# Nine hat products of a strip divided between VectorE and GpSimd, and a second group of sampled values taken by VectorE, in a fused residual network with a deformable convolution

## What is computed

```python
def _deform_conv(x, offsets, w_def, stride, pad):
    off = offsets.reshape(B, K2, 2, Ho, Wo)
    dy, dx = (off[:, :, 0], off[:, :, 1])
    ...
    py = hs[None, None, :, None] + iy[None, :, None, None] + dy
    px = ws[None, None, None, :] + ix[None, :, None, None] + dx
    y0 = jnp.floor(py)
    x0 = jnp.floor(px)
    wy = py - y0
    wx = px - x0
    ...
    val = gather(y0, x0, (1 - wy) * (1 - wx))
    val = val + gather(y0, x0 + 1, (1 - wy) * wx)
    val = val + gather(y0 + 1, x0, wy * (1 - wx))
    val = val + gather(y0 + 1, x0 + 1, wy * wx)
    return jnp.einsum('bckhw,ock->bohw', val, w_def.reshape(Cout, C, K2))
offsets = _conv2d(x, w_off, b_off, STRIDE, PAD)
...
x = x + _L0_conv_ref(_gn(x), ...)
x = x + _L1_conv_ref(_gn(x), ...)
```

## Time and profile before

| | us |
|---|---|
| median of 3 runs (lowest, highest) | 1302.1 (1301.43, 1303.63) |
| the profiled execution's own time | 1300.54 |
| its span, first to last instruction | 1298.7 |

### The profile page before, as it was taken

How to read it: one execution, slowest core, us unless ns; L and a number is a source line. 1 busy time by engine, 2 the same in 40 slices (tenths; PEclk the granted TensorE clock), 3 DMA queues, 4 the chain that set the end, 5 groups by cost and what they waited for, 6 DMA issues and landing times.

```text
span 1298.7 us, 42328 instructions
## 1 busy us (share of the span) xinstructions
PE 1061.0 (82%) x17334; PEld 681.5 (52%) x17334; DVE 887.3 (68%) x1379; ACT 669.6 (52%) x901; POOL 61.9 (5%) x87
## 2 busy tenths in 40 slices
PE   0799999987593999999965867888878887888884
PEld 0234546664241454447742325777767776776764
DVE  4877762334985878751517947888878887888870
ACT  0532433112175334332113476888878887888871
POOL 0000000000051000000000350000000000000000
PEclk9999999999795999999998876999999998999998
DMA  9000022110585000202305345443433443444331
GB/s 198 1 1 2 2 94 67 42 27 4 134 202 150 1 1 2 91 6 67 67 1 123 93 142 152 137 133 112 135 117 110 122 135 102 125 128 124 114 86 36
DMA packets 96466, 109.83 MB, mean 85 GB/s; under 512 B 10127, under 2 KB 85735, under 8 KB 94616
## 3 DMA queue, kind: packets, MB, share of 16 engines
q1 hardware_dynamic: 87816, 101.73, 28.6%
q10 hardware_dynamic: 8464, 5.37, 1.9%
HBM read 74.85 MB, written 32.22 MB: 82 GB/s over the span
## 4 chain that ended last, share of the span: by engine, by line
issue 44%; PE 41%; DVE 5%; POOL 2%; ACT 2%; DMA 2%; SPq 1%; POOLq 0%; DVEq 0%; ACTq 0%
PE psum L832 22%; PE psum L901 13%; PE psum L965 3%; DMA xm<-x 2%; DVE v L1626 2%; PE psum L942 1%; SPq L529 1%; POOL offr L2003 1%; POOL offp L2007 1%; ACT xm L1377 1%; PE psum L979 1%; PE psum L923 1%; DVE xm L1792 1%; PE psum L932 1%; DVE stats L1795 1%
## 5 line engine op out<-in xcount | busy, mean ns | idle before, releaser
L832 PE MATMUL psum<-v,u 64*64 64x512 f32 x3072 | 336.8, 597 | 17.7 <-DVE v L1626 12.7
L1449 ACT ACTIVATE dist<-psum 128x1024 f32<-128x1024 f32 x288 | 288.9, 1025 | 54.1 <-PE psum L1028 39.1
L832 PEld LDWEIGHTS psum<-v,u 64*64 64x64 f32 x3072 | 148.2, 134 | 204.8 <-issue 188.1
L1839 DVE TENSOR_SCALAR dist<-dist 128x1024 f32<-128x1024 f32 x288 | 201.9, 701 | 77.1 <-ACT dist L1449 75.5
L1075 PE MATMUL psum<-hat,win 64*64 64x144 f32 x4096 | 199.5, 318 | 32.7 <-DVE outt L1875 18.2
L1849 DVE TENSOR_TENSOR hat<-dist 128x512 f32<-128x512 f32 x288 | 194.8, 685 | 0.3
L1148 PE MATMUL psum<-val,wdefs 64*64 64x256 f32 x1944 | 166.0, 395 | 33.0 <-ACT val L1452 24.1
L1075 PEld LDWEIGHTS psum<-hat,win 64*64 64x64 f32 x4096 | 152.7, 135 | 66.3 <-issue 64.7
L1452 ACT ACTIVATE val<-psum 128x864 f32<-128x864 f32 (+3 forms) x230 | 146.5, 675 | 34.6 <-PE psum L1075 22.7
L1028 PE MATMUL psum<-offs,sels 61*64 61x256 bf16 x2304 | 139.1, 284 | 21.4 <-issue 11.2
L1148 PEld LDWEIGHTS psum<-val,wdefs 64*64 64x64 f32 x1944 | 91.1, 136 | 48.1 <-issue 44.6
(11 more groups left out here) (144 smaller groups left out, 1097.2 us busy)
## 6 DMA issues: line engine op xcount, KB each, us to landing
win<-pixd SPq DMA_DIRECT2D x256, 68.0 KB
win<-pixd SPq DMA_DIRECT2D x128, 136.0 KB
raw<-x SPq DMA_DIRECT2D x16, 512.0 KB, 7.4
x1d<-xm SPq DMA_DIRECT2D x16, 512.0 KB, 6.0
pixd<-turned SPq DMA_DIRECT2D x64, 128.0 KB, 3.9
x1t<-x1d SPq DMA_DIRECT2D x63, 128.0 KB, 2.8
out<-outt SPq DMA_DIRECT2D x63, 128.0 KB, 2.6
offd<-offp SPq DMA_DIRECT2D x48, 128.0 KB
```

The lines of the kernel that those rows point to most:

```text
L832: mm = pe.matmul(o, u4[half, i, v, ky, :], V[half, at:at + CHUNK, cg, v, :], start=start, stop=stop, skip_group_check=True)
L1449: act.activation(dist_at(j, n), psum[:, slot:slot + 2, :], ACT.Abs).then_inc(dist_abs, 1)
L1839: dve.tensor_scalar(d, d, 1.0, 1.0, ALU.min, ALU.subtract).then_inc(hats_made, 1)
```

## The change

Three of the nine products of a strip (taps 1, 4 and 7) are issued by POOL, with a semaphore of their own (`prod_pool`); DVE keeps six. Whoever waited for products now waits for the one of the two semaphores that counts that product, and PE's group 0 for both. Group 4 of the values, 128x576, goes from ACT to DVE, behind the hats of tap 8. The core of the diff:

```diff
-ACT_GROUPS = [0, 1, 3, 4, 5]
-DVE_GROUPS = [2]
+ACT_GROUPS = [0, 1, 3, 5]
+DVE_GROUPS = [2, 4]
+POOL_UNITS = [1, 4, 7]
+DVE_UNITS = [0, 2, 3, 5, 6, 8]
...
+        def product_made(s, n):
+
+            if n in POOL_UNITS:
+                return prod_pool, len(POOL_UNITS) * s + (POOL_UNITS.index(n) + 1)
+            return prod_dve, len(DVE_UNITS) * s + (DVE_UNITS.index(n) + 1)
...
                 if g == 0:
                     pe.wait_ge(win_in[j], count)
-                    pe.wait_ge(prod_dve, UNITS * (s + 1))
+                    pe.wait_ge(prod_dve, len(DVE_UNITS) * (s + 1))
+                    pe.wait_ge(prod_pool, len(POOL_UNITS) * (s + 1))
...
-                    act.wait_ge(prod_dve, UNITS * q + (m_ + 1))
+                    act.wait_ge(*product_made(q, m_))
...
                     if not last:
                         hats(s + 1, 1 - j, n)
-                        if n > 0:
+                        if n - 1 in DVE_UNITS:
                             product(s + 1, 1 - j, n - 1)
...
             for n in range(UNITS):
                 hats(0, 0, n)
-                product(0, 0, n)
+                if n in DVE_UNITS:
+                    product(0, 0, n)
...
+            def products(s, j):
+
+                for n in POOL_UNITS:
+                    if n == POOL_UNITS[0] and not (isinstance(s, int) and s < 2):
+                        pool.wait_ge(vals_made, GROUPS * (s - 1))
+                        settled(pool)
+                    pool.wait_ge(hats_made, UNITS * s + (n + 1))
+                    pool.tensor_tensor(*product_of(j, n), ALU.mult).then_inc(prod_pool, 1)
+
+            products(0, 0)
+            products(1, 1)
+            with pool.Fori(1, STRIPS // 2) as h:
+                products(2 * h, 0)
+                products(2 * h + 1, 1)
```

More of the change, by code:

```diff
@@ L370, in build @@
         prod_dve = sem("prod_dve")
+        prod_pool = sem("prod_pool")
         vals_made = sem("vals_made")
@@ L488, in general, with product_of @@
                     end()
+        def product_made(s, n):
+            if n in POOL_UNITS:
+                return prod_pool, len(POOL_UNITS) * s + (POOL_UNITS.index(n) + 1)
+            return prod_dve, len(DVE_UNITS) * s + (DVE_UNITS.index(n) + 1)
+        def product_of(j, n):
+            d = dist_at(j, n)
+            lo = TAP_PITCH * n + n % K
+            to = hat[:, j, lo:lo + BANK].rearrange("p (b n) -> p b n", b=IMAGES)
+            return to, d[:, :, 0:PS * HALF_W], d[:, :, PS * HALF_W:]
         def group_taken(s, g):
@@ L1499, in edge_absolute @@
                 if e:
-                    act.wait_ge(prod_dve, UNITS * STRIPS)
+                    act.wait_ge(prod_dve, len(DVE_UNITS) * STRIPS)
+                    act.wait_ge(prod_pool, len(POOL_UNITS) * STRIPS)
                 act.activation(dist[:, DIST_RING - 1, :, 0:K * W0], psum[:, 0:2, 0:K * W0], ACT.Abs).then_inc(edge_abs, 1)
@@ L1845, in product @@
                 dve.wait_ge(hats_made, UNITS * s + (n + 1))
[L1846 to L1849, removed]
+                dve.tensor_tensor(*product_of(j, n), ALU.mult).then_inc(prod_dve, 1)
             def edge_product(e):
```

## The result

| | before | with the change |
|---|---|---|
| median of 10 runs, us | 1301.81 | 1304.96 |
| lowest, highest | 1296.02, 1303.63 | 1303.02, 1306.8 |
| profiled execution: span, us | 1298.7 | 1304.2 |

The ratio to before is 1.0028, with a 95% interval from 1.0014 to 1.0041: slower, by 2 to 5 us. The forecast was slower by 13.5. The direction held and the size did not: 3.15 us is a quarter of what I had summed.

What follows compares the result with a forecast made beforehand. Bound: a chain of engines waiting in turn. A strip loses 0.50 - 0.10 = 0.40 us, 12.0 us over 30 strips, plus 1.5 at the start: 1300.5 + 13.5 = 1314.0, plus 1.6 to the median, 1315.5 us; range 1300 to 1328.

Steps and rivals of the forecast that it cites:

- What bounds the kernel: Engines wait in turn; PE stands still 18.2 us for DVE's result and 24.1 us for ACT's last copies.
- The price of POOL's product: On DVE ahead of the result: 0.60 us removed, 1.10 added by blocked hats, result 0.50 late in each strip.
- the upper bound for two products: A product on DVE and one on POOL were priced as excluding each other, for the whole 1.16 us.
- the first rival: On DVE and POOL: two products run side by side, only hats are blocked; 1302 us, chance 0.12.
- The second: Rival: POOL gets in only where DVE waits, so the result comes 0.60 us earlier; 1291.5 us, chance 0.13.
- The third: Rival: DVE becomes the bound, all three blocks count, 0.9 to 1.0 us a strip; about 1331 us, chance 0.15.
- Taps 4 and 7 at nothing: On DVE behind the result: the blocked hats of taps 5 and 8 added nothing to the strip's sum.
- The products together: POOL's three products: 0.50 us for each of 30 strips, plus 1.5 us for blocked hats ahead of any strip.
- Group 4, "I credit 0.1 us a strip": At the strip's end ACT loses one copy, about 0.62 us; 0.1 was credited, the other 0.52 covered by PE.
- is done in time: DVE's copy of group 4 (0.7 us), behind the hats of tap 8, would be done at about 1017.3.
- The sign: For the whole kernel: slower at chance 0.72, faster 0.17, same 0.11.

Runs made afterwards that it cites:

- e7: Kernel before, with POOL multiplying the hats of tap 1 once more into an unread buffer, nothing taken from DVE; 1328.94 us against 1302.08, ratio 1.0199.
- e8: e5 with the result moved one place forward on DVE, ahead of the product of tap 3; ratio to before 0.9931.
- e4: Changed kernel with only the products of taps 4 and 7 on POOL and group 4 back on ACT; ratio to before 1.0034.
- e1: Changed kernel with group 4 back on ACT, so only the products of taps 1, 4 and 7 move to POOL; 1313.52 us against 1300.92, ratio 1.0085.
- e2: Kernel before with only the copy of group 4 moved to DVE, all nine products staying on DVE; 1308.3 us against 1300.92, ratio 1.0061.
- e5: e2 with DVE copying group 4 directly behind the hats of tap 8, ahead of the product of tap 7; ratio to before 0.9987.

## Why the prediction was right and wrong

**What bounds the kernel: right.** The time is decided on DVE's order between the hats of tap 1 and the result, and by PE's waits for result and copies. e7 and e8 show that from both sides: 1.09 us more there cost 26 us, one place less brought about 7.

**The price of POOL's product: right, to 0.01 us.** I summed 1.10 added, 0.60 removed, 0.50 late. Measured: 1.10 (e7), and 5.31 against 4.82, 0.49. The choice of the upper bound for two products, argued from doubled reading, was right too (1.63 us at 778.34), so the first rival fell. (It is the first rival, not the second as the prediction has it, that goes with two products side by side.) The second fell with it: POOL never waited longer than one product of DVE. The third did not come either: DVE still waits 51.9 us for ACT between the first and the 30th result.

**Taps 4 and 7 at nothing: nearly right.** e4 measures 4 us (2 to 7) for them.

**The products together: over-priced.** Without the credit for group 4 my sum has 16.5 us for them. e1 has just them and measures 11 (8 to 14).

**Group 4, "I credit 0.1 us a strip": mis-sized, and priced in the wrong way. This is the step that failed.** Two things went wrong there.

First the size. The gain behind the result is 0.16 in A and 0.37 in B, not 0.1. In the changed kernel ACT is done with its copies earlier behind PE's edge columns than in the earlier trace rows. The timelines of PE and of ACT at the end of a strip A:

```profile
1019.35 0.41 PE L1104 MATMUL psum<-hat,win 64*64 64x12 f32 x14
...
1019.56 0.21 PE L1104 MATMUL psum<-hat,win 64*64 64x12 f32 x2
```

```profile
1019.83 1.05 ACT L1469 ACTIVATE val<-psum 128x576 f32<-128x576 f32 x3 [0.33 <-PE psum L1104]
1020.77 1.94 ACT L1466 ACTIVATE dist<-psum 128x1024 f32<-128x1024 f32 x2
```

The edge matmuls end at 1019.77. ACT is at the next first distance 1.00 us behind that, at 1020.77. In the trace of before it was 1.16 behind, at 1017.27, from 1016.11:

```profile
1017.27 5.20 ACT L1449 ACTIVATE dist<-psum 128x1024 f32<-128x1024 f32 x5
```

Second, and more, I added terms that do not add. I let ACT's gain count on PE's weighing ("group 5 and the edges are made by PE only at 1016.11"), and wrote that DVE's copy "is done in time". It is not quite: the weighing stands 0.53 and 0.87 us behind the first distance, where it stood 0.00 and 0.43. The gain goes to ACT's next distances, and the later weighing makes the distances of the taps behind late. Alone that eats up the gain (e2). In the change the hats of tap 2 are blocked by POOL in just that stretch, and the late distances arrive while they are blocked. The two delays lie side by side, so the change pays the longer of the two, 5.31 us, and keeps the gain. In strip A there is a third thing: before, the median way to the result was 4.97 and not the 4.82 of the strip that I read, since there too DVE waited for distances now and then; so the block cost A 0.34 and not 0.49.

The corrected sum by the table: a pair of strips 0.34 + 0.49 for the block, less 0.16 and 0.37 behind the result, is 0.30 for two strips; the medians of the periods themselves give 0.15 (29.84 - 29.69), since medians of parts do not add exactly. That is 2.3 to 4.5 us over 15 pairs. Measured: 3.15. My sum had 0.80 for a pair, 1.00 for the block less 0.20.

Means over the 29 strips, from the third on, do add, and show both halves of the account. For a pair, A and B together:

| kernel | hats of tap 1 to result, us | result to next first distance, us |
|---|---|---|
| before | 10.05 | 16.26 |
| e1 products only | 10.92 | 16.20 |
| e2 group 4 only | 10.93 | 15.68 |
| the change | 10.91 | 15.69 |

The products alone lengthen the first way by 0.87, group 4 alone by 0.88, and both together by 0.86: they hide each other. The gain behind the result is group 4's, 0.57 in the change. The rest, 0.86 less 0.57, is 0.29 for a pair and 4.3 us over 15 pairs. In strips wholly at 2.4 GHz the first way is, in the same order, 9.82, 10.79, 10.45 and 10.62 us, again no longer with both than with the products alone.

**The sign.** Slower was right, at 0.72, and what made it so is the block. But the range, from 1300 to 1328, was wide and its point was carried by one strip's timeline; a strip B in which the wait for the result was only 0.52 us, and the scatter of the periods, were there to be read.

## What to carry to other kernels

Before an elementwise instruction goes to GpSimd, look at what VectorE does beside it: if it reads two SBUF inputs, as the products here, or is a tensor_scalar that takes 1024 fp32 values in 0.69 us, as the hats, the two take turns, and the move costs more than it saves (1.10 against 0.60 us here). In a pipeline of engines that wait in turn, price two edits together, at the point where their delays meet: delays in the same stretch hide each other, and an engine that runs ahead of its feeder can lose again what it gained. Where an instruction feeds a waiting engine, its place in an in-order stream can count more than the engine it runs on: one place of the result was worth about 7 us here (e5 against e8), while products on an idle engine made no kernel faster than the one that has the same order without them (e5, e8). And before a timed difference of half a percent is put down to an order, the granted clock of both kernels has to be the same: that of e2 was not.

## What the runs showed of the hardware that I had not expected

POOL's product was recorded with 1.64 to 1.67 us in the changed kernel, in all 96 cases, and not with the 1.16 of the earlier trace rows. It is not slower. In 93 of the 96 it asks while DVE's product is under way, in the other 3 while hats are, and by the start times of all 96 it ends 1.12 to 1.15 us behind the end of that instruction (1010.41 against 1009.28); usually it asks 0.16 us behind the start of DVE's product, and once in e7 it asked 0.05 behind it:

```profile
779.22 0.69 DVE L1853 TENSOR_TENSOR hat<-dist 128x512 f32<-128x512 f32 x1
779.83 1.75 DVE L1843 TENSOR_SCALAR dist<-dist 128x1024 f32<-128x1024 f32 x1
```

```profile
779.27 1.77 POOL L2024 TENSOR_TENSOR scr<-dist 128x512 f32<-128x512 f32 x1 [1.96 <-DVE dist L1843]
```

There it took 1.77 and again ended 1.13 behind DVE's product (781.04 against 779.91). So a recorded duration of GpSimd holds its wait for VectorE. DVE's next hats start in the records at 779.83, 0.08 before the product's end, and still POOL gets its turn first; in none of the rows shown here did a second instruction of DVE pass a waiting POOL.
